# Up products of a mixture-of-experts layer in three fp16 passes, in a two-layer decoder with a planned order

## The reference

```python
def expert_layer(h):            # h: tokens x 128, normed
    logits = h @ gate_w.T                       # 8 experts
    top, idx = top_k(logits, 2); p = softmax(top)
    for e in range(8):
        hidden = relu(h @ w1[e].T + b1[e])      # up product, 128 -> 512
        y = hidden @ w2[e].T + b2[e]            # down product, 512 -> 128
        out += weight_of(e, idx, p) * y
```

## Time and profile before

| | us |
|---|---|
| median of 3 runs | 396.71 |
| lowest, highest | 393.55, 396.99 |
| the profiled execution | 397.64 |
| its span, first to last instruction | 395.9 |
| PE busy | 343.0 |
| DVE busy | 220.4 |
| ACT busy | 217.7 |
| POOL busy | 84.3 |
| mean granted TensorE clock, share of full | 0.922 |

### The profile page before, as it was taken

The page is one execution under the profiler, slowest core; times in us unless marked ns, Lnnn a source line. Parts: engine busy times, 40 slices in busy tenths (PEclk is TensorE's granted clock), DMA queues, the critical chain, the costliest instruction groups (busy, mean ns, idle before and its releaser), DMA issues.

```text
span 395.9 us, 8364 instructions
## 1 busy us (share of the span) xinstructions
PE 343.0 (87%) x3048; PEld 239.5 (60%) x3048; DVE 220.4 (56%) x642; ACT 217.7 (55%) x419; POOL 84.3 (21%) x186
## 2 busy tenths in 40 slices
PE   1647998786978958787999999999999999999995
PEld 0432455453966846453556677884767888668755
DVE  3778558884366567978346687856321456122112
ACT  1348887769768464356054775445756444531440
POOL 3757877323333052300002200000000000000000
PEclk9995999999999866968567999999999999999999
DMA  7920000000000460000000000000000000000000
GB/s 207 418 88 2 2 2 2 2 2 0 2 2 1 170 256 2 0 2 0 2 2 0 2 2 2 2 0 2 3 2 15 2 0 15 0 2 0 2 1 28
DMA packets 4186, 12.31 MB, mean 31 GB/s; under 512 B 490, under 2 KB 2802, under 8 KB 3122
## 3 DMA queue, kind: packets, MB, share of 16 engines
q1 hardware_dynamic: 4146, 11.77, 8.0%
HBM read 11.24 MB, written 0.52 MB: 30 GB/s over the span
## 4 chain that ended last, share of the span: by engine, by line
PE 67%; DVE 14%; ACT 9%; issue 5%; DMA 2%; POOL 2%; SPq 1%; DVEq 0%; ACTq 0%; POOLq 0%
PE double L1599 14%; PE single L1610 12%; PE single L1272 6%; PE single L1264 5%; PE outs L1369 4%; PE double L1320 3%; DVE mx L1115 3%; PE double L1316 2%; PE double L1610 2%; ACT xn L803 2%; ACT region_p L844 2%; DVE mxc L1102 2%; DMA row<-in_row 2%; PE outs L1377 2%; PE double L1485 1%
## 5 line engine op out<-in xcount | busy, mean ns | idle before, releaser
L844 ACT ACTIVATE region_p<-double 128x1024 f32<-128x1024 f32 x64 | 64.3, 1028 | 25.6 <-PE double L1320 18.5
L918 ACT ACTIVATE hidden<-double,col 128x256 f32<-128x256 f32 (+1 forms) x96 | 45.3, 546 | 52.2 <-PE double L1599 52.2
L1599 PE MATMUL double<-xnT,w 128*128 128x256 f32 (+1 forms) x192 | 59.4, 455 | 0.0
L1244 DVE SCALAR_TENSOR_TENSOR x<-single,comb,x 128x128 f32<-128x128 f32 x54 | 15.8, 345 | 65.9 <-PE single L1610 65.8
L1610 PEld LDWEIGHTS single<-w,hidden 128*128 128x128 f32 x432 | 50.0, 192 | 2.8 <-issue 2.3
L1610 PE MATMUL single<-w,hidden 128*128 128x128 f32 x432 | 50.8, 276 | 0.0
L684 POOL TENSOR_SCALAR rstd<-mv 128x2 f32<-128x2 f32 x24 | 5.5, 228 | 209.9 <-DVE mv L979 209.3
L1599 PEld LDWEIGHTS double<-xnT,w 128*128 128x128 f32 x192 | 34.5, 190 | 16.8 <-issue 13.7
L1115 DVE TENSOR_REDUCE mx<-double 128x4 f32<-128x1024 f32 (+1 forms) x24 | 29.4, 1226 | 8.8 <-PE double L1485 8.2
L1369 PE MATMUL outs<-region_p,vst 128*32 128x256 f32 x256 | 22.4, 436 | 0.0
L1102 DVE TENSOR_REDUCE mxc<-double 128x16 f32<-128x1024 f32 x16 | 19.6, 1224 | 3.5 <-PE double L1464 3.1
(11 more groups left out here) (251 smaller groups left out, 650.4 us busy)
## 6 DMA issues: line engine op xcount, KB each, us to landing
w<-in_w1a SPq DMA_DIRECT2D x2, 1024.0 KB, 11.0
w<-in_w2a SPq DMA_DIRECT2D x2, 1024.0 KB, 12.6
w<-in_w1b SPq DMA_DIRECT2D x2, 1024.0 KB, 7.7
w<-in_w2b SPq DMA_DIRECT2D x2, 1024.0 KB, 10.5
row<-in_row SPq DMA_DIRECT2D x1, 800.0 KB, 7.4
wb<-in_wb SPq DMA_DIRECT2D x1, 709.0 KB, 8.5
x<-in_x SPq DMA_DIRECT2D x4, 128.0 KB, 2.8
out<-x SPq DMA_DIRECT2D x4, 128.0 KB, 1.9
```

The source lines that it names most:

```text
L844: a.activation(probs[:, slot("prob", key), :], psum(step), ACT.Exp, scale=SCALE).then_inc(psum_done[PSUM.slot(step)], 1)
L918: a.activation(dst[:, c, 0:w], psum(step)[:, k * w:(k + 1) * w], ACT.Relu, bias=colv("b1m", e * HC + c)).then_inc(psum_done[PSUM.slot(step ...
L1244: ins = v.scalar_tensor_tensor(x[:, t, :], psum(step)[:, i * P:(i + 1) * P], comb[:, t, e:e + 1], x[:, t, :], ALU.mult, ALU.add)
L1599: ins = mm(o if w == T else two(o), w1[:, e, c * P:(c + 1) * P], n6T, start=True, stop=True)
```

## The change

- The up products of the mixture: tokens and weights are each split into a high and a low fp16 part, the weights scaled by 64 first. Each product is the sum of three fp16 passes in PSUM: high by high, high weight by low token, low weight by high token. The width of each pass is as before.
- New steps `ws(e)`: ACT writes the high part of expert e's weights, DVE the low part, in the place of the expert before (for e = 0 in the place of bias rows no longer needed). The first can run when the weights of layer 1 are there. New steps `xs(b)`: POOL writes the two parts of batch b's normed tokens into the unused half of `xnT`, after `tr(6, b)`.
- The scale is undone by the combine weights (a scale in existing instructions of `gb` and `gc`); the biases are scaled once by a small ACT copy.
- Down products stay fp32.
- `BY_VECTOR` lists 45 steps whose evacuation or norm is done by DVE instead of ACT: 12 `mup`, 6 `tq` and `tqm`, 5 `oc`, 5 `ou`, 5 `tr`, 2 `tr2`, 2 `tr3`, 3 `lnb`, 2 `gc`, 2 `ml`, and `kct(4)`. `kct(1)` goes from DVE to ACT.
- The costs in `the_steps` are changed, and the order of all 521 steps is another.

The core of the diff:

```diff
-BY_SCALAR = (2, 3, 4)
+SHIFTED = (2, 3, 4)
 SCALE = float(1.0 / (HD ** 0.5))
 MAXDIV = 64.0
+WSCALE = 64.0
...
+VECTOR = {"tr": 0.35, "tr2": 0.75, "tr3": 0.37, "ou": 0.35, "ml": 0.35, "tq": 0.7, "tqm": 0.7, "tk4": 0.7,
+          "kct": 0.7, "oc": 0.6, "gc": 0.41, "mup": 1.2}
+
+
+BY_VECTOR = (
+    40, 66, 73, 76, 91, 93, 98, 100, 115, 138, 152, 167, 169, 190, 191, 217, 235, 241, 247, 251,
+    264, 277, 289, 291, 295, 298, 328, 353, 358, 382, 393, 400, 448, 456, 457, 462, 463, 468, 469,
+    472, 474, 475, 491, 497, 499,
+)
...
+        if len(steps) in BY_VECTOR:
+            parts = [("D", vector_time(step)) if engine == "A" else (engine, t) for engine, t in parts]
...
-        add(("kct", l), [("kck", l), ("casts", 0)], ("P", 0.45), ("D", 0.7))
+        add(("kct", l), [("kck", l), ("casts", 0)], ("P", 0.50), ("A", 1.09))
...
-                add(("mup", g, e, q), [("tr", 6, b) for b in group], ("P", 1.71),
-                    ("A", 1.36 if n == 2 else 1.6),
+                add(("mup", g, e, q), [("xs", b) for b in group] + [("ws", e)], ("P", 1.36),
+                    ("A", 1.26 if n == 2 else 1.57),
                     behind=[("mup", g, e, q - 1) if q else e and ("mup", g, e - 1, n - 1)])
...
+    for e in range(NE):
+        add(("ws", e), [("tr3", 0), ("tr3", 1), e and ("ws", e - 1)] + [("lnb", 1, b) for b in every] +
+            [("q1", b) for b in every], ("A", 0.63), ("D", 0.69))
+    for b in every:
+        add(("xs", b), [("tr", 6, b)], ("G", 1.15))
...
+NUMBER = {step: n for n, step in enumerate(STEPS)}
+
+
+def by_vector(step):
+
+    return NUMBER[step] in BY_VECTOR or step[0] == "lnb" and step[1] not in SHIFTED
...
+        w1s = [(row[:, 0:512] if e == 0 else w1[:, e - 1, :]).bitcast(F16).rearrange(
+            "p (s n) -> p s n", s=2) for e in range(NE)]
...
+        xs = xnT[:, 0, :].bitcast(F16).rearrange("p (m q s t) -> p q s m t", m=2, q=2, s=2)
...
+                elif kind == "xs":
+
+                    written(pool, ("tr", 6, b))
+                    hi, lo = (xs[:, b % 2, n, b // 2, :] for n in range(2))
+                    src = xnT[:, 1, toks(b)]
+                    then(g.tensor_copy(hi, src))
+                    then(g.tensor_tensor(lo, src, hi, ALU.subtract), "x_split")
...
+                if by_vector(step):
+                    continue
...
-                    evac(step, combT[:, :], psum(step)[0:NE, 0:T])
+                    evac(step, combT[:, :], psum(step)[0:NE, 0:T], WSCALE)
+                elif kind == "ws":
+                    e = step[1]
+                    act.wait_ge(sem(f"w1b_loaded{e // 4}"), 16)
+                    if e == 0:
+
+                        act.wait_ge(sem("stack_ready"), max(count(STACKS, ("q1", n)) for n in range(NB)))
+                        act.wait_ge(sem("x_biased"), max(biased(("lnb", 1, n)) for n in range(NB)))
+                        act.wait_ge(sem("col_loaded"), 16)
+                        then(a.activation(b1s[:, :], part(col, COL, "b1m"), ACT.Copy, scale=WSCALE),
+                             "biases_scaled")
+                    else:
+                        act.wait_ge(sem("w_split"), e)
+                    then(a.activation(w1s[e][:, 0, :], w1[:, e, :], ACT.Copy, scale=WSCALE), "w_high")
...
-                    if q == 0:
-                        read_by_tensor(act, "hidden", (g, e))
-                    act.wait_ge(sem("col_loaded"), 16)
+                    read_by_tensor(act, "hidden", (g, e))
+                    act.wait_ge(sem("biases_scaled"), 1)
                     act.wait_ge(psum_full, PSUM.full(step))
                     dst, w, n = hidden[:, slot("hidden", (g, e))], T * len(GROUPS[g]), fills(step)
                     for k in range(n):
                         c = n * q + k
                         a.activation(dst[:, c, 0:w], psum(step)[:, k * w:(k + 1) * w], ACT.Relu,
-                                     bias=colv("b1m", e * HC + c)).then_inc(
+                                     bias=b1s[:, e * HC + c:e * HC + c + 1]).then_inc(
...
+            def evac(key, out_ap, in_ap, scale=None):
+
+                dve.wait_ge(psum_full, PSUM.full(key))
+                gives(key, v.tensor_copy(out_ap, in_ap) if scale is None else
+                      v.tensor_scalar(out_ap, in_ap, scale, None, ALU.mult))
+
+            def stack_evac(step, dst):
+
+                evac(step, dst[:, :, :].rearrange("p g (i t) -> p i g t", i=2),
+                     psum16(step).rearrange("p (i g t) -> p i g t", i=2, g=4))
...
+                elif kind in ("tq", "tqm") and by_vector(step):
+                    if step[1] == 5:
+                        read_by_tensor(dve, "qcT", b)
+                        stack_evac(step, qcT[:, slot("qcT", b)])
+                    else:
+                        stack_evac(step, qT[:, :, toks(b)])
...
+                elif kind == "mup" and by_vector(step):
+                    _, g, e, q = step
+                    read_by_tensor(dve, "hidden", (g, e))
+                    dve.wait_ge(sem("biases_scaled"), 1)
+                    dve.wait_ge(psum_full, PSUM.full(step))
+                    dst, w, n = hidden[:, slot("hidden", (g, e))], T * len(GROUPS[g]), fills(step)
+                    for k in range(n):
+                        c = n * q + k
+                        v.tensor_scalar(dst[:, c, 0:w], psum(step)[:, k * w:(k + 1) * w],
+                                        b1s[:, e * HC + c:e * HC + c + 1], 0.0,
+                                        ALU.add, ALU.max).then_inc(
+                            psum_done[PSUM.slot(step)], 1)
...
-                    then(v.tensor_scalar(w, e, 1.0, None, ALU.add))
+                    then(v.tensor_scalar(w, e, WSCALE, WSCALE, ALU.mult, ALU.add))
...
+                elif kind == "ws":
+
+                    e = step[1]
+                    dve.wait_ge(sem("w_high"), e + 1)
+                    then(v.scalar_tensor_tensor(w1s[e][:, 1, :], w1[:, e, :], WSCALE, w1s[e][:, 0, :],
+                                                ALU.mult, ALU.subtract), "w_split", wait=False)
...
-                        written(pe, ("tr", 6, b))
-                    pe.wait_ge(sem(f"w1b_loaded{e // 4}"), 16)
-                    dst, w, n = take(step), T * len(GROUPS[g]), fills(step)
-                    b = GROUPS[g][0]
-                    n6T = (xnT[:, 1, toks(b)] if w == T else
-                           xnT[:, 1, :].rearrange("p (m q t) -> p q m t", m=2, q=2)[:, b])
+                        pe.wait_ge(sem("x_split"), count(("xs",), ("xs", b)))
+                    pe.wait_ge(sem("w_split"), e + 1)
+                    dst, w, n, b = take(step), T * len(GROUPS[g]), fills(step), GROUPS[g][0]
                     for k in range(n):
                         o, c = dst[:, k * w:(k + 1) * w], n * q + k
-                        ins = mm(o if w == T else two(o), w1[:, e, c * P:(c + 1) * P], n6T,
-                                 start=True, stop=True)
+                        for m, (w_part, x_part) in enumerate(((0, 0), (0, 1), (1, 0))):
+                            ins = mm(o if w == T else two(o), w1s[e][:, w_part, c * P:(c + 1) * P],
+                                     xs[:, b, x_part] if w > T else xs[:, b % 2, x_part, b // 2, :],
+                                     start=m == 0, stop=m == 2)
```

155 lines of the change are left out of this document (99 added, 56 removed), and 53 rows, old and new, of the table ORDER_TABLE.

## The result

The changed kernel's median is 385.8 us (four executions, 382.58 to 392.03), against 396.85 for the kernel before in the same comparison: a ratio of 0.965 with a 95% interval of 0.954 to 0.977. In a later comparison its eight executions had a median of 386.16 (382.47 to 391.71), ratio 0.969 (0.962 to 0.976). The profiled execution took 383.04 us, its span 381.3. Forecast: 383, range 375 to 392.

What follows compares the result with a forecast made beforehand. PE was taken as the bound, full from 228 us on, with DVE nearly full earlier. 395.9 - 12.6 - 4 - 1.5 + 3 + 1.5 = 382.3 us of span, forecast 383; own range 379 to 387, with rivals 375 to 392.

Steps and rivals of the forecast that it cites:

- Passes, -12.6: Up products: three fp16 passes replace fp32, saving 0.41 us per wide step and 0.38 per narrow, 12.6 us in all.
- 576 records: Expected sign in the profile after: 576 up-product records, with 1.30 to 1.40 us from one mup to the next step.
- DVE's evacuations of `mup`, costed at nothing: Twelve up-product evacuations moved to DVE, at most 16.6 us, costed at nothing because DVE had free time late in the order.
- more than 53: Sign of failure: last group, first mup to last matmul, takes more than 53 us; 51.3 was expected, without waits.
- Start, -4: Kernel start: reordered early work lets the rotation and first score come sooner, a gain of 4 us, bounds 0 and -5.
- the 17.2 for the rotation's product: Kernel start: the rotation's first table product could start at 17.2 us instead of 21.07, once rotary tables are ready at 16.85.
- the gain gone by 98 us: Sign of failure: the time gained at the kernel's start is lost again by 98 us.
- 60 to 98, -1.5: From 60 to 98 us: about 4 us more DVE work, 6 less ACT; net gain 1.5 us, bounds +2.5 and -4.
- 147 to 185, +3: From tr(4,1) to sc(4,1,0): some 5.6 us of extra DVE work ahead of PE and ACT costs 3 us, bounds 0 and +6.
- the extra DVE work is taken in: Rival, chance 22%: the +3 and +1.5 vanish and 2 us of the half-speed stretch return, giving 377 us.
- 228 to 268, +1.5: From 228 to 268 us: PE and DVE nearly level, so small waits on PE cost 1.5 us, bounds 0 and +3.5.
- The clock: Rival, chance 7%: short PE waits between 228 and 268 us bring the 1.2 GHz level, giving 393 or even 401 us.

Runs made afterwards that it cites:

- the split of the two halves: Changed kernel with each last-group up product evacuated by ACT (first 512 columns) and DVE (second) together; median 387.09 us.
- the second profile: The changed kernel itself, unchanged, profiled again in a later comparison; span 386.9 us, median of its eight executions 386.16 us.
- the order alone: Changed kernel with new order and DVE table kept, up products back in fp32 without weight and token splits; median 391.31 us, ratio to before 0.9945.
- the memset first: Changed kernel with POOL's 3.52 us memset of the values' buffer put before x arrives, the context's memset behind the rotary tables; median 389.23 us.

## Why the prediction was right, step by step

The time was met (383 against 385.8), by a sum in which one gain did not come, two losses did not come, and one loss was missing. Passes and their size were understood; that the rest cancelled is luck.

- **Passes, -12.6.** A wide `mup` was put at 1.32 us and is 1.31; a narrow one at 1.38 and is 1.31 to 1.41. Held against the same order in fp32 they give 6.2 us for the narrow ones (6.1 in the sum) and 5.3 for the wide ones (6.6): 11.5. The missing 1.3 in the wide ones belongs to the next point. The "576 records" was a miscount: an fp16 matmul is one record, not two, and the three groups of L1731 hold the 96 x 3 = 288.
- **DVE's evacuations of `mup`, costed at nothing: the mis-sized term.** I argued from DVE's free share in the last group, 49 of 62 us. But PE does not wait for a share; it waits for one bank, and a bank is emptied by one engine in 1.42 us while a `mup` is 1.31. That is 2.2 us, as the split of the two halves gave back. To the end of the last matmul the last group took 55.8 us, so the sign that the prediction named for its own failure, more than 53, is there. 2.5 of them are mdown(2,7) and gd(0), which the order put there; the other 53.3 still stand against 51.3 forecast. The price was also too low: 745 ns, not 690.
- **Start, -4: wrong, +0.8 at the first score.** The rule on DVE and POOL had been applied to the one cast that the earlier trace rows show under the memset, and not to what the new order puts in its place, a norm that is held for 3.65 us. With the memset out of the way the first score still came 2.6 us later than the 25.5 forecast: the 17.2 for the rotation's product took the tables as its only condition, and left out ACT's squares and the 1.7 us of DVE work between them and the product. The sign that the prediction named for its own failure, the gain gone by 98 us, is there: 0.7 us are there at the first `fup`, and the stretch from the first score on gives 1.6.
- **60 to 98, -1.5.** From the first score to the first `fup`: 70.8 us before, 69.2 after. Right, and not by the clock: the second profile, at 0.90 in this stretch against 0.94 before and 1.00 in the first, takes 69.2 too.
- **100 to 143, put at nothing.** From the first `fup` to tr(4,1) it is 46.1 us before and 43.9 after. The sum has no term for these 2.2 us. With the order alone it is 45.3, and so it is in the changed kernel with the memset first: the same 247 or so records take 43.9 us at a granted clock of 0.92 or 0.93 and 45.2 to 45.5 at 0.88 or 0.89. So 1.3 of the 2.2 hang on the clock of the execution; the rest may be the order's.
- **147 to 185, +3: wrong, -0.3.** The terms add up to 5.4 us, not 5.6. Counting DVE's work by its place in the order took in some 3.3 us that nothing waited for, and left out that the order had taken 4.2 us of DVE's pauses out. `ws` in itself was right: 2.4 us here when it is left out. The rival "the extra DVE work is taken in" (377) describes this stretch better.
- **228 to 268, +1.5: not there.** PE is 39.73 of 40 busy, with DVE at 36.11, 2 us more than reckoned. Nearly level engines hardly produced waits, for the next 53 us neither (52.73 busy).
- **The clock.** It was 1.00 from the first `mup` to the last matmul in every profile, so the rival (drops behind the first `mup`) did not come. But the prediction treated the half-speed stretch ahead of it as the same before and after. Between two profiles of one kernel it makes 6 us, more than any step of the sum but the first.

Summed as the landmarks have it: -0.7 to the first `fup`, -2.6 from there to sc(4,1,0), +2.2 from there to the first `mup`, and behind it -11.5 for the passes and -2.1 for the order (105.7 + 57.2 us before, 100.05 + 60.8 with the order alone). That is -14.7, against 14.6 between the spans. The +2.2 and the -2.1 are in part one thing, the eight steps that the order moves from one side of the first `mup` to the other. The second profile of the same kernel gives -9.0, its difference in the third term (+8.3; 0.4 of it come back by the first `fup`). The forecast, 383, is what the first profile took. That the median of 386 has more of the half-speed stretch in it is likely and not shown. The clock was in my range as a rival of 7%, placed where it did not act.

## What to carry over

Price an evacuation by the bank, not by the engine's free share: what one engine needs to empty it, against what PE needs to fill it; if they are close, give its halves to two engines. When work is moved in time, look at what the other engines hold in the new place, since a long memset of POOL stopped the casts and norms of DVE that came under it (not a `tensor_tensor`). Where executions of one kernel differ by more than the effect in question, compare landmark to landmark, and see where the granted clock fell before crediting an edit.
